# Attention's TensorE loop: one chunk a pass in place of two, the ring's half read from a word

## The reference

```
xl = (x @ W_l).reshape(n, H, C)
xr = (x @ W_r).reshape(n, H, C)
feat = xl[src] + xr[dst]
feat = jnp.where(feat >= 0, feat, NEG_SLOPE * feat)
logits = jnp.einsum('ehc,hc->eh', feat, att)
seg_max = jax.ops.segment_max(logits, dst, num_segments=n)
ex = jnp.exp(logits - seg_max[dst])
seg_sum = jax.ops.segment_sum(ex, dst, num_segments=n)
alpha = ex / (seg_sum[dst] + 1e-16)
msg = alpha[:, :, None] * xl[src]
out = jax.ops.segment_sum(msg, dst, num_segments=n)
```

## Time and profile before

| | us |
|---|---|
| Median of three runs | 2590.89 |
| Lowest, highest | 2586.61, 2599.18 |
| The profiled execution's own time | 2595.44 |
| Its span | 2593.6 |
| PE busy | 2026.5 (78%) |
| DVE busy | 1562.9 (60%) |
| POOL busy | 1332.7 (51%) |
| ACT busy | 1263.8 (49%) |

### The profile page before, as it was taken

The page is one execution under the profiler, slowest core; times in us unless marked ns, Lnnn a source line. Parts: engine busy times, 40 slices in busy tenths (PEclk is TensorE's granted clock), DMA queues, the critical chain, the costliest instruction groups (busy, mean ns, idle before and its releaser), DMA issues. The chain is left out here.

```text
span 2593.6 us, 44433 instructions
## 1 busy us (share of the span) xinstructions
PE 2026.5 (78%) x9489; PEld 1670.2 (64%) x9490; DVE 1562.9 (60%) x3500; ACT 1263.8 (49%) x3196; POOL 1332.7 (51%) x1263
## 2 busy tenths in 40 slices
PE   3965888887888888788887887873876619999994
PEld 2754666666766676666666766652765517888884
DVE  6955777777777777777777777889455410111110
ACT  2542656665665665566565665652545402222221
POOL 3345566665565666656565665619004552444442
PEclk9987999999898999999999899995875559999997
DMA  7676666666666666666666666725502346666665
GB/s 210 233 246 178 193 190 188 176 195 181 186 177 183 189 189 187 185 186 191 181 177 192 188 191 170 201 67 173 164 17 96 120 124 155 144 138 143 142 145 139
DMA packets 255242, 436.15 MB, mean 168 GB/s; under 512 B 41849, under 2 KB 126754, under 8 KB 255062
## 3 DMA queue, kind: packets, MB, share of 16 engines
q1 hardware_dynamic: 173082, 264.66, 33.2%
q0 software_dynamic: 66272, 154.09, 24.6%
q10 hardware_dynamic: 15836, 16.81, 2.1%
HBM read 370.08 MB, written 71.74 MB: 170 GB/s over the span
## 5 line engine op out<-in xcount | busy, mean ns | idle before, releaser
L816 POOL DMA_INDIRECT ring<-xl_rows,a_idx x928 | 925.3, 997 | 602.8 <-issue 250.2
L1150 PE MATMUL a_o_ps<-ring,a_hot_e 128*128 128x264 f32 x1856 | 540.8, 418 | 201.0 <-DVE acc L1025 168.1
L1137 PE MATMUL a_f_ps<-a_xr_w,a_hot_n 128*128 128x268 f32 x1856 | 590.7, 402 | 45.7 <-ACT a_lg L901 18.4
L1139 PE MATMUL a_f_ps<-ring,ident 128*128 128x264 f32 x1856 | 608.3, 411 | 0.0
L1150 PEld LDWEIGHTS a_o_ps<-ring,a_hot_e 128*128 128x128 f32 x1856 | 360.3, 203 | 308.7 <-issue 224.2
L995 DVE SCALAR_TENSOR_TENSOR a_pos<-a_f_ps,att_ext 128x528 f32<-128x528 f32 x464 | 325.2, 701 | 380.2 <-remote 200.0
L1137 PEld LDWEIGHTS a_f_ps<-a_xr_w,a_hot_n 128*128 128x128 f32 x1856 | 371.6, 205 | 124.3 <-issue 55.7
L901 ACT COPY a_lg<-a_f_ps 128x8 f32<-128x8 f32 x464 | 79.5, 171 | 548.5 <-DVE a_pos L995 437.6
L1005 DVE TENSOR_REDUCE a_lg<-a_pos 128x8 f32<-128x528 f32 x464 | 323.3, 697 | 1.4 <-remote 0.6
L1013 DVE TENSOR_TENSOR ring<-ring (+1 forms) x464 | 316.5, 682 | 0.1
L1139 PEld LDWEIGHTS a_f_ps<-ring,ident 128*128 128x128 f32 x1856 | 313.5, 204 | 0.0
(11 more groups left out here) (318 smaller groups left out, 2178.5 us busy)
## 6 DMA issues: line engine op xcount, KB each, us to landing
a_xr_w<-xr_rows SPq DMA_DIRECT2D x464, 268.0 KB
a_rel_bc<-rel_rows SPq DMA_DIRECT2D x116, 256.0 KB
x_w<-in_L_ffn_W_dram SPq DMA_DIRECT2D x56, 512.0 KB
ring<-xl_rows,a_idx POOLq DMA_INDIRECT x928
ring<-disp_rows SPq DMA_DIRECT2D x56, 257.0 KB
xr_rows<-xr_parts SPq DMA_DIRECT2D x50, 268.0 KB, 2.1
xl_rows<-xl_sb SPq DMA_DIRECT2D x50, 132.0 KB, 1.9
j_xl<-xl_rows SPq DMA_DIRECT2D x25, 264.0 KB, 2.8
```

What stands on the lines that cost most here:

```text
L816: nc.gpsimd.indirect_dma_start(xl_e[:, p * T + 2 * h + u, :], None, k.xl_rows, bass.IndirectOffsetOnAxis(ap=idx[:, p, 2 * h + u:2 * h + u ...
L1137: nc.tensor.matmul(f_ps[:, g, u, 0:XRW], hot_n[:, j % 2, 2 * g + u, :], xr_w[:, h % XR, a, :].bitcast(F32R), start=(a == 0), stop=False)
L1139: last = nc.tensor.matmul(f_ps[:, g, u, 0:XW], k.ident[:, :], xl_e[:, p * T + 2 * h + u, :], start=False, stop=True)
L1150: last = nc.tensor.matmul(o_ps[:, hh % 2, 0:XW], hot_e[:, j % 2, 2 * g + u, :], xl_e[:, pp * T + 2 * hh + u, :], start=(u == 0), stop=(u = ...
```

## The change

PE uses `steps_alone` too, with one chunk in its body and 26 passes. `step` builds two views of the ring, `halves[0]` for the chunk's own half and `halves[1]` for the other. Outside the loop these are fixed. Inside, `ring_half` loads two words of `parity` into PE's registers at the top of each pass, and the views are addressed by them. `logits_of` and `sums_of` take the view in place of the number of the half.

```diff
@@ -1125,7 +1125,7 @@
 
             @block.tensor
             def _(pe):
-                def logits_of(c, p, h):
+                def logits_of(c, half, h):
                     j, g = h // 2, h % 2
                     if g == 0:
                         pe.wait_ge(hot_n_ready, c * QUADS + (j + 1))
@@ -1136,11 +1136,11 @@
                         for a in range(PARTS):
                             nc.tensor.matmul(f_ps[:, g, u, 0:XRW], hot_n[:, j % 2, 2 * g + u, :], xr_w[:, h % XR, a, :].bitcast(F32R),
                                              start=(a == 0), stop=False)
-                        last = nc.tensor.matmul(f_ps[:, g, u, 0:XW], k.ident[:, :], xl_e[:, p * T + 2 * h + u, :],
+                        last = nc.tensor.matmul(f_ps[:, g, u, 0:XW], k.ident[:, :], half[:, 2 * h + u, :],
                                                 start=False, stop=True)
                     last.then_inc(f_done, 1)
 
-                def sums_of(cc, pp, hh):
+                def sums_of(cc, half, hh):
                     j, g = hh // 2, hh % 2
                     if g == 0:
                         pe.wait_ge(hot_e_ready, cc * QUADS + (j + 1))
@@ -1148,7 +1148,7 @@
                     wait_past(pe, added, cc * NU + (hh - 1))
                     for u in range(2):
                         last = nc.tensor.matmul(o_ps[:, hh % 2, 0:XW], hot_e[:, j % 2, 2 * g + u, :],
-                                                xl_e[:, pp * T + 2 * hh + u, :], start=(u == 0), stop=(u == 1))
+                                                half[:, 2 * hh + u, :], start=(u == 0), stop=(u == 1))
                     last.then_inc(sum_done, 1)
 
                 def softmax(cc, part):
@@ -1187,19 +1187,24 @@
                         nc.tensor.matmul(sm[:, 2:2 + H], spot[:, 0], faded[:, :], start=True, stop=False)
                         nc.tensor.matmul(sm[:, 2:2 + H], spot[:, 1], ones[:, :], start=False, stop=True).then_inc(faded_turned, 1)
 
-                def step(c, p):
+                def step(c):
+                    if isinstance(c, int):
+                        halves = [xl_e[:, (c + b) % 2 * T:(c + b) % 2 * T + T, :] for b in range(2)]
+                    else:
+                        halves = [xl_e.rearrange("p (s t) w -> p s t w", s=2)[:, bass.ds(s, 1)].rearrange("p o t w -> p (o t) w")
+                                  for s in ring_half(mybir.EngineType.PE, c)]
                     for h in range(NU):
                         if has_logits(c):
-                            logits_of(c, p, h)
+                            logits_of(c, halves[0], h)
                         if softmax_in(c) and h in (0, 2, 4):
                             softmax(c - 1, h // 2)
                         sums = behind(c, h, SUM)
                         if sums:
-                            sums_of(sums[0], (p + sums[1]) % 2, sums[2])
+                            sums_of(sums[0], halves[sums[1] % 2], sums[2])
                         if softmax_in(c) and h in (5, 6, 8):
                             softmax(c - 1, (5, 6, 8).index(h) + 3)
 
-                steps(pe, step)
+                steps_alone(pe, step)
 
 
 def batch_scale(nc, link, stats, par, scale, tmp, root):
```

## The result

The changed kernel takes **2610.64 us** (median of 6 runs, 2604.58 to 2621.13), the kernel before 2592.66 us on the same chip (6 runs, 2580.31 to 2599.18). The ratio is 1.0076, interval 1.0047 to 1.0105: slower by 0.76%, about 18 us. That lies inside the range of 2582 to 2629, but on the side to which the prediction gave 0.34.

A forecast was written before the change was run, and what follows sets the result against it. PE and DVE wait for each other in the loop, neither full, with outside stalls of 3 to 6 us. Terms 8.5 + 0.5 = +9 us gave 2604 on the profiled execution, forecast 2600 us as median; range 2582 to 2629.

The forecast's parts named there:

- What the change takes away: PE's loop text falls from two chunks to one; no instruction transfers saved in the loop, 0 counted, -2 us as the end.
- the third rival's price: Each PE loop-back fetches instructions: 13 more fetches, about 1 us each, giving 2613; chance 0.03.
- Term 1, the size of the gap: Top of PE's loop: load 1.05 plus register operations 0.25 makes 1.3 us a seam, 26 times, 33.8 us raw.
- Term 1, its cover: PE's wait at L1163 hides 15 of 29.9 us, leaving 17 us for 26 seams; +8.5 us after later waits.
- I take half: Of the 17 us left after L1163, half is hidden in PE's later waits: +8.5 us, ends 0 and 33.8.
- The other piece of that step: The remaining delay can be hidden again in PE's waits for DVE at L1150, over 6 us a chunk.
- Terms 2 and 3: 44 more register operations a chunk for L1139, L1150 addresses: 0.5 us; SP's loads and POOL's gathers, run ahead: 0 us.
- the gap is not absorbed: Before L1137 of unit 0 DVE waits for PE at once, later work moves too; full price 33.8 us, about 2625; chance 0.30.
- The clock that this rival had added: After long PE stands, L1150 matmuls run at 1.2 GHz; about 2 us a spell, five new ones add 10.
- a "remote" total that moves by over 20 us: Sign that the prediction is wrong: DVE's "remote" waits in the loop, 151.4 us before, move by over 20 us.

The follow-up runs named there:

- made stalls: SP starts a small copy after three units' logits a chunk, DVE waits for its landing; put into several kernels; kernel before with it: 2507.13 us against 2263.85.
- the pair with made stalls: Kernel before and the change, both with SP's copies that DVE waits for: 2507.13 and 2539.15 us.
- the old loop with made stalls: Kernel before, two chunks in PE's body, plus SP's copies that DVE waits for: 2507.13 us against 2263.85, ratio 1.1084.

## Why the prediction came out as it did

**What the change takes away: right.** No instruction transfer in the loop, before or after. (Where this part of the prediction speaks of "the third rival's price", the rival that it means, the fetches, is the fourth of its list.)

**Term 1, the size of the gap: right.** Forecast 1.3 us a seam, from ACT's load and three register operations. The load took 0.536 us where 0.54 was assumed, and the distance from L1150 to L1137 grew by 0.89 us on average on the first chip and by 1.31 with the made stalls. At some seams of the first chip next to nothing of it showed (0.81 us at two of them). One premise was off: the loop-back that was read, with 0.80 us against 0.70, was taken to say that the branch had used up the sequencer's lead, but with made stalls and no load the branch and the addresses together add 0.03 us.

**Term 1, its cover: the step that failed.** "A gap of 1.3 us is hidden 7 x 1.3 + 13 x 0.45 = 15 of 29.9 us" expected the wait at L1163 to shrink from 29 us by about half. It is 29.3. Only the short waits went, 5.8 to 0.6 us; the long ones, which end with DVE's L1005, fell at other seams with other lengths, 28.7 us in 8 where it had been 23.2 in 7. Then "I take half": of 33.8 us raw the sum kept 8.5, and the medians differ by 18, the chunks of the profiled execution 18.3 (0.70 us of 1.3 a seam). The other piece of that step held: idle time ahead of L1150 did fall, by 0.52 us a chunk, but longer matmuls took its place in the profiled execution.

**Terms 2 and 3, right at near 0.** The addresses and the branch together: -0.04% on a chip without stalls and -1.0 us under made stalls. A forecast of 0.5 us is not distinguishable from that. On the first chip they were not run apart. Its trace of the change bounds them in part: of the 1144 address operations in the loop four lasted over 150 ns longer than usual, 1.3 us in sum.

**The rival "the gap is not absorbed" fits the number better than the forecast did.** Its bounds, 2606 to 2635, hold 2610.6, and its mechanism (DVE waits at once, its later work moves too) is seen in the pair with made stalls, at 32.0 us, against the full price of 33.8 in the prediction. On the first chip it is argued and not shown. DVE's waiting grew by 0.6 us a chunk in total there, but not ahead of unit 0, and no kernel without the load, or with the seam elsewhere, ran there. That the 18 us come from the load rests on the pairs with made stalls, whose longest stall ends in another way. The clock that this rival had added is in the trace too: 0.92 to 0.91, some 0.6 us of PE a chunk; the six executions suggest that a part of it belongs to the profiled one alone.

**The signs.** I called a "remote" total that moves by over 20 us a sign against the argument. It moved by 29.6, to DVE's waits for PE. That sign was badly chosen: the two are one quantity under two names, and its sum moved by 9.8 us.

The range held the result, but the forecast of +9 us stood on a cover that wasn't there, and half of what was taken as lost.

No version beats the kernel before. Two equal it with a loop of one chunk, without stalls and with made ones: the half computed from the pass number, and the seam put at L1163.

## What to carry to other kernels

In this kernel a load by PE's sequencer at the top of the loop cost anything from nothing (where PE stood at that place for a gather) to nearly its full time (a load of two words with what hangs on it, 1.2 to 1.3 us a pass, with made stalls). So put the seam just ahead of a wait for another engine, or form the value from the loop's own counter, which cost nothing here. Cover should be counted seam by seam on the engine that is next in the cycle, not from a sum of waits: in the old loop with made stalls it was 0.6 us ahead of DVE's unit 0, and one look at one seam says so. A delay can be paid nearly in full although both engines are idle for a good part of the time: with the change and made stalls PE was busy 883.70 and DVE 836.44 of 1100 us. And a stall that is made on purpose needs its own check of what ends it.

## What the runs showed of the hardware that was not expected

**The same kernel takes 2591 us on one chip and 2261 us on another.** Whether it is the chip or the hour can't be told, since none of the four chips of the experiments was used twice at different times. No profile of the kernel before was kept on a faster chip; beside the kernel with the half from the pass number there, 273 of 335 us are in the attention's loop (52.9 against 42.4 us a chunk), 23 in its first two chunks and 39 in the routing. On the slower chip the profile shows idle time of DVE of up to 5.8 us under the name "remote". Operations of SP's sequencer are stretched there too: in the loop of the kernel before, 321 of 2542 lasted over 150 ns longer than the median of their kind, 188 us in sum, and in the loop on the faster chip none of 2539. Line 834, the kernel before:

```profile
L834 SPq TENSOR_LOAD <-row_words x29: 16/442/725, 172.6 to 1640.7; - x29
L834 SPq SEQ_ASSERT  x29: 10/18/719, 173.3 to 1641.4; - x29
```

and on the faster chip, the kernel with the half from the pass number:

```profile
L834 SPq TENSOR_LOAD <-row_words x29: 437/442/492, 172.4 to 1348.8; - x29
L834 SPq SEQ_ASSERT  x29: 18/18/37, 173.2 to 1349.5; - x29
```

An assertion of 18 ns at the median takes up to 719 ns on one and never more than 37 on the other. The cause wasn't found, and that the stretched operations and the "remote" waits have one cause is not shown. For this change it decides the verdict: +0.76% on the first chip, +0.05% (-0.06 to +0.16) on the other.

**The clock follows the stalls.** The loop has a granted clock of 0.92 with them and 1.00 without; with made stalls on a chip without others it is 0.93 with the old loop, 0.92 with the change. In the trace of the change, after a stand of 2.79 us at L1150 the four matmuls took 2.12 us, in place of 1.05 (the level of 1.2 GHz, not 2.4):

```profile
679.67 2.12 PE L1150 MATMUL a_o_ps<-ring,a_hot_e 128*128 x4 [2.79 <-DVE acc L1025]
...
687.28 1.05 PE L1150 MATMUL a_o_ps<-ring,a_hot_e 128*128 x4
```

So a stall of this length costs PE more than its own time.
